# A four-layer graph attention kernel: transposes of x one quad ahead, rows of attention scaled one slot ahead, values a group ahead, last norms in another order

## What is computed

```python
x = _layernorm(x + _L0_gnn_ref(x, adj, ...))   # 4 heads of 64, leaky_relu 0.01, softmax over adj, elu
x = _layernorm(x + _L1_gnn_ref(x, adj, ...))   # 4 heads of 64, leaky_relu 0.2
x = _layernorm(x + _L2_gnn_ref(x, adj, ...))   # 1 head of 256; then three gated dense blocks and two norms
x = _layernorm(x + _L3_gnn_ref(x, adj, ...))   # h = tanh(x W + b); weights exp(h a), masked by adj
# in each: h = x @ W; scores from h; att = softmax(mask(leaky_relu(s_i + s_j))); out = att @ h
```

## Time and profile before

| | |
|---|---|
| median of 3 runs | 3059.14 us (3057.73 to 3062.9) |
| the profiled execution, its own time | 3061.66 us |
| its span | 3059.9 us |
| mean granted clock of PE | 0.993 of full |

### The profile page before, as it was taken

The page is one execution under the profiler, slowest core; times in us unless marked ns, Lnnn a source line. Parts: engine busy times, 40 slices in busy tenths (PEclk is TensorE's granted clock), DMA queues, the critical chain, the costliest instruction groups (busy, mean ns, idle before and its releaser), DMA issues.

```text
span 3059.9 us, 65157 instructions
## 1 busy us (share of the span) xinstructions
PE 2955.5 (97%) x24628; PEld 2582.1 (84%) x24628; DVE 2140.8 (70%) x3855; ACT 1919.1 (63%) x3414; POOL 1174.4 (38%) x1559
## 2 busy tenths in 40 slices
PE   7899999999989999999999999999999999889998
PEld 6899999999979999999997877887778778655555
DVE  5998887888878888888886556665666666562245
ACT  4777898999978999999995545444445444430000
POOL 0661365642226656564121023333323333444222
PEclk9999999999999999999999999999999999989999
DMA  8567100000100000000010000000000000000001
GB/s 286 202 209 250 48 11 11 14 11 15 60 12 14 12 12 13 12 13 11 14 34 12 4 1 4 4 1 4 1 4 4 1 1 1 2 1 1 1 17 39
DMA packets 41912, 104.55 MB, mean 34 GB/s; under 512 B 9856, under 2 KB 23424, under 8 KB 33536
## 3 DMA queue, kind: packets, MB, share of 16 engines
q1 hardware_dynamic: 39616, 101.61, 10.0%
q10 hardware_dynamic: 2112, 0.52, 0.1%
HBM read 97.73 MB, written 4.39 MB: 33 GB/s over the span
## 4 chain that ended last, share of the span: by engine, by line
PE 77%; DVE 3%; ACT 2%; POOL 1%; issue 1%; POOLq 0%; DVEq 0%; ACTq 0%
PE bank L1359 17%; PE bank L1356 16%; PE bank L1414 15%; PE bank L1452 12%; PE bank L1362 10%; PE bank L1441 2%; PE bank L1289 2%; PE bank L1428 1%; PE bank L1569 0%; ACT above L964 0%; DVE rings L1784 0%; ACT rings L1099 0%; DVE rings L1787 0%; ACT values L861 0%; DVE sums L1938 0%
## 5 line engine op out<-in xcount | busy, mean ns | idle before, releaser
L1356 PE MATMUL bank<-values,rings 128*128 128x195 bf16 x8192 | 1414.5, 247 | 37.6 <-DVE rings L1787 25.2
L1359 PE MATMUL bank<-values,rings 128*128 128x195 bf16 x8192 | 1414.6, 249 | 0.0
L964 ACT ACTIVATE above<-srow,kpass 128x512 fp8e4<-128x512 f32 x2032 | 1279.7, 709 | 128.5 <-DVE rings L1787 121.8
L1356 PEld LDWEIGHTS bank<-values,rings 128*128 128x128 fp8e4 x8192 | 806.4, 98 | 47.4 <-issue 45.3
L1359 PEld LDWEIGHTS bank<-values,rings 128*128 128x128 fp8e4 x8192 | 789.1, 96 | 0.6
L1784 DVE TENSOR_TENSOR rings<-rings,above 128x512 uint32<-128x512 uint32 x512 | 400.2, 782 | 192.3 <-PE bank L1359 168.5
L1052 ACT ACTIVATE values<-srow,cmul 128x512 f32<-128x512 f32 x256 | 205.8, 814 | 428.3 <-PE bank L1452 427.3
L1787 DVE TENSOR_TENSOR rings<-rings 128x512 uint32<-128x512 uint32 x512 | 429.7, 839 | 17.3
L1452 PE MATMUL bank<-hv,values 128*128 128x257 f32 x1792 | 420.6, 380 | 0.0
L1452 PEld LDWEIGHTS bank<-hv,values 128*128 128x128 f32 x1792 | 334.9, 190 | 69.9 <-issue 25.2
L1362 PE MATMUL bank<-values,rings 128*128 128x390 bf16 x1920 | 320.3, 329 | 11.9 <-DVE values L1820 11.9
(11 more groups left out here) (223 smaller groups left out, 3479.1 us busy)
## 6 DMA issues: line engine op xcount, KB each, us to landing
arena<-in_adj_dram SPq DMA_DIRECT2D x64, 1024.0 KB, 5.0
srow<-src_dram SPq DMA_DIRECT2D x69, 256.0 KB, 3.2
x<-in_x_dram SPq DMA_DIRECT2D x4, 1024.0 KB, 11.4
out_dram<-x SPq DMA_DIRECT2D x7, 512.0 KB, 2.9
arena<-in_L_gnn_fe_w_dram SPq DMA_DIRECT2D x2, 512.0 KB, 6.7
arena<-in_L_gnn_W_hz_dram SPq DMA_DIRECT2D x1, 1024.0 KB, 7.6
arena<-in_L_gnn_g_w_dram SPq DMA_DIRECT2D x1, 1024.0 KB, 10.8
weights<-in_L_gnn_W_dram SPq DMA_DIRECT2D x3, 256.0 KB, 3.9
```

What stands on the lines that cost most here:

```text
L964: last = act.activation(above[:, k % 2, q, :], srow[:, par, :], ACT.Relu, scale=BIG, bias=kpass[:, p % 2, k * Q + q:k * Q + q + 1], satura ...
L1356: pe.matmul(acc[:, 0:KW], pos[:, k % 2, q, :].bitcast(FP8)[:, rows], v[:, 0:KW], start=start, stop=final, skip_group_check=True)
L1359: last = pe.matmul(acc[:, KW:2 * KW], neg[:, k % 2, q, :].bitcast(FP8)[:, rows], v[:, KW:2 * KW], start=False, stop=final, skip_group_chec ...
```

## The change

Five things move; no arithmetic is added or removed.

1. Layers 0 to 2: a second buffer for the transposed x, and the transposes of quad q+1 (`x_across`) stand between the products of quad q: four after its second tile, four after its fourth. ACT's copies of them (`copy_xT_half`) stand behind the copies of h of the second and fourth tile. PE waits for ACT's copy of h by the tile and no longer by the quad. In layer 1, elu of the last quad and `first_keys` come one quad later.
2. Layer 0: POOL makes the values of the third head one group further ahead of the quotients.
3. Layer 2: `scale_rows` moves on ACT from slot 1, behind `whT`, to slot 0, behind that slot's first rows.
4. End of layer 2: `s_wfix` is signalled before the tail, without waiting for layer 3's vector, which has a semaphore of its own at its first use. The last pair's `g2_product`, `gate_tanh` and `gate_in` come after layer 3's fifth product, its tanh, and `tanh_in(4)`.
5. The end: the first three steps of quad 5's norm come before the last full group's sums, quad 6's first steps after the first addition of `last_rows`, and its last steps between the statistics and the normalising of tile 0 of quad 7.

```diff
-        xT = tiles_room[:, 0:QT * F]
+        xT_rooms = (tiles_room[:, 0:QT * F], tiles_room[:, QT * F + CHUNK * 2 * C:2 * QT * F + CHUNK * 2 * C])
...
+        xT = [xt.rearrange("p (t k n) -> p t k n", t=QT, k=2) for xt in xT_rooms]
...
-        s_wfix = sem("weights_fixed")
+        s_wfix, s_a3 = sem("weights_fixed"), sem("layer3_vector_loaded")
...
                     sp.wait_ge(E.uT, 4 * EG)
-                    load_vector(avec[:, 0, :], A["L3_gnn_a"][:, 0])
+                    sp.dma_start(avec[:, 0, :], A["L3_gnn_a"][:, 0].partition_broadcast(P)).then_inc(s_a3, 16)
...
-        loaded_weights = [16 * 4, 16 * 13, 16 * 16, 16 * 19]
+        loaded_weights = [16 * 4, 16 * 13, 16 * 16, 16 * 18]
...
                 values_of(0, 2, 1)
+                values_of(0, 2, 2)
                 for g in range(2, NG):
-                    values_of(0, 2, g)
+                    if g + 1 < NG:
+                        values_of(0, 2, g + 1)
                     quotient(0, 1, g, g % 2)
...
+                make_rstd(4, QUADS - 3)
                 quotient(3, PASSES[3] - 1, NG - 2, 0)
-                make_rstd(4, QUADS - 3)
                 make_rstd(4, QUADS - 2)
...
-            def copy_quad_xT(l, q):
-                for half in range(2):
-                    act.wait_ge(s_xtps, q * 2 + (l * 2 * QUADS + half + 2))
-                    act.activation(xT[:, 2 * half:2 * half + 2].rearrange("p t k n -> p (t k n)"), bank[half][:, :],
-                                   ACT.Copy).then_inc(s_xt, 1)
+            def copy_xT_half(l, q, half):
+                act.wait_ge(s_xtps, q * 2 + (l * 2 * QUADS + half + 2))
+                act.activation(xT[q % 2][:, 2 * half:2 * half + 2].rearrange("p t k n -> p (t k n)"), bank[half][:, :],
+                               ACT.Copy).then_inc(s_xt, 1)
...
+                    if i % 2 == 1 and q + 1 < QUADS:
+                        copy_xT_half(l, q + 1, i // 2)
...
                         relus(i * SLOTS + slot)
+                        if slot == 0 and i % 2 == 0 and old:
+                            scale_rows(g - 1)
                         if slot == 1 and i > 0:
                             act.wait_ge(E.n1, i + 1)
                             act.activation(whT.rearrange("p k n -> p (k n)"), ps_a, ACT.Copy).then_inc(E.whT, 1)
-                            if old and i % 2 == 0:
-                                scale_rows(g - 1)
...
-                gate_tanh(EG - 1)
                 for r in (4, 5):
                     copy_h(r)
                     copy_xT(r + 2)
                     tanh3(r)
+                    if r == 4:
+                        gate_tanh(EG - 1)
                 copy_h(6)
...
+                    for half in range(2):
+                        copy_xT_half(l, 0, half)
                     for q in range(QUADS):
-                        copy_quad_xT(l, q)
-                        if l == 1 and q + AHEAD + 3 < QUADS:
-                            elu_exp(q + AHEAD + 3)
+                        if l == 1 and q in (0, 2):
+                            elu_exp(AHEAD + 3 + q // 2)
...
+            def x_across(l, q, half):
+                if l == 0 and half == 0 and q % (QUADS // X_PIECES) == 0:
+                    pe.wait_ge(s_x[q // (QUADS // X_PIECES)], 16)
+                for i in (2 * half, 2 * half + 1):
+                    if l > 0:
+                        pe.wait_ge(s_xmade, q * QT + (NORMS[l] * T + i + 1))
+                    for k in range(2):
+                        last = pe.transpose(bank[half][:, (i % 2 * 2 + k) * P:(i % 2 * 2 + k + 1) * P],
+                                            x[:, q * QT + i, k * P:(k + 1) * P], ident[:, :])
+                last.then_inc(s_xtps, 1)
             def dense(l, q):
-                for half in range(2):
-                    for i in (2 * half, 2 * half + 1):
-                        if l > 0:
-                            pe.wait_ge(s_xmade, q * QT + (NORMS[l] * T + i + 1))
-                        for k in range(2):
-                            last = pe.transpose(bank[half][:, (i % 2 * 2 + k) * P:(i % 2 * 2 + k + 1) * P],
-                                                x[:, q * QT + i, k * P:(k + 1) * P], ident[:, :])
-                    last.then_inc(s_xtps, 1)
                 if q == 0:
+                    for half in range(2):
+                        x_across(l, 0, half)
                     pe.wait_ge(s_wfix, l + 1)
-                pe.wait_ge(s_h, q * QT + (l * T + 1))
+                    pe.wait_ge(s_h, l * T + 1)
                 width = F + 2 * H
                 for i in range(QT):
+                    if q > 0:
+                        pe.wait_ge(s_h, (q - 1) * QT + (l * T + i + 2))
                     if l > 0 and q == 0 and 2 + i == GT:
                         pe.wait_ge(s_sums, l * SUMS + 1)
                     pe.wait_ge(s_xt, q * 2 + (l * 2 * QUADS + i // 2 + 1))
                     for k in range(2):
-                        last = pe.matmul(bank[2 + i][:, 0:width], xT[:, i, k, :], weights[:, k, 0:width],
+                        last = pe.matmul(bank[2 + i][:, 0:width], xT[q % 2][:, i, k, :], weights[:, k, 0:width],
                                          start=(k == 0), stop=(k == 1))
                     last.then_inc(s_hps, 1)
+                    if i % 2 == 1 and q + 1 < QUADS:
+                        x_across(l, q + 1, i // 2)
...
-                g2_product(EG - 1)
                 for r in range(4, EG):
                     product3(r)
                     if r + 2 < EG:
                         across3(r + 2)
+                    if r == 4:
+                        g2_product(EG - 1)
...
-                    if l == 1 and q == AHEAD + 1:
+                    if l == 1 and q == AHEAD + 2:
                         first_keys(1)
...
+                chain.enter(NG - 3, 2)
+                for k in (2, 3, 4):
+                    output_norm(QUADS - 3, k)
                 evacuate(3, 0, 0, last_pass + NG - 1)
-                chain.enter(NG - 3, 2)
-                for k in (2, 3, 4, 6, 7):
+                for k in (6, 7):
                     output_norm(QUADS - 3, k)
                 chain.leave(NG - 2)
-                for k in (2, 3, 4, 6, 7):
-                    output_norm(QUADS - 2, k)
                 last_rows()
...
                 link(dve.tensor_tensor(xq, xq, hq, ALU.add))
+                for k in (2, 3, 4):
+                    output_norm(QUADS - 2, k)
                 for it in range(GT):
...
                     dve.bn_aggr(st[:, 6:8], st[:, 0:6]).then_inc(s_var, 1)
+                    if it == 0:
+                        for k in (6, 7):
+                            output_norm(QUADS - 2, k)
                     dve.wait_ge(s_rstd, QUADS * (NORMS[4] + 1) + it)
                     dve.tensor_scalar(tile, tile, st[:, 6:7], st[:, 9:10], ALU.subtract, ALU.mult).then_inc(s_xmade, 1)
...
+                    if r == 0:
+                        dve.wait_ge(s_a3, 16)
...
+                dve.wait_ge(s_w, loaded_weights[3])
+                dve.memset(credits[:, 11:12], 0.0).then_inc(s_wfix, 1)
                 fused_stats(EG - 3)
...
                 g_norm(EG - 2, 0)
-                dve.wait_ge(s_w, loaded_weights[3])
-                dve.memset(credits[:, 11:12], 0.0).then_inc(s_wfix, 1)
                 x_norm(EG - 3)
                 g_norm(EG - 2, 1)
...
                 fused_norm(EG - 2)
+                tanh_in(4)
                 gate_in(EG - 1)
-                tanh_in(4)
                 tanh_scores(4)
```

More of the change, by code:

```diff
@@ L222, in gnn_kernel @@
         tiles_room = vroom[:, T * KW:]
-        xT = tiles_room[:, 0:QT * F]
+        xT_rooms = (tiles_room[:, 0:QT * F], tiles_room[:, QT * F + CHUNK * 2 * C:2 * QT * F + CHUNK * 2 * C])
         vtmp_dve = tiles_room[:, QT * F:QT * F + CHUNK * 2 * C].rearrange("p (a n c) -> p a n c", a=2, c=C)
         ex = [vroom[:, i * QT * F:(i + 1) * QT * F].rearrange("p (t f) -> p t f", t=QT) for i in range(3)]
-        xT = xT.rearrange("p (t k n) -> p t k n", t=QT, k=2)
+        xT = [xt.rearrange("p (t k n) -> p t k n", t=QT, k=2) for xt in xT_rooms]
         class Room:
@@ L1646, in _ @@
                     for q in range(QUADS):
-                        if l == 0 and q % (QUADS // X_PIECES) == 0:
-                            pe.wait_ge(s_x[q // (QUADS // X_PIECES)], 16)
                         dense(l, q)
```

## The result

The median went from 3060.01 us (3057.73 to 3062.9, 4 runs) to 3026.82 (3026.59 to 3030.63, 4 runs), 33.2 us less; the ratio is 0.9894, 95% interval 0.9877 to 0.9911. The forecast was 3029.5, between 3022 and 3039. The profiled execution took 3027.04 us, span 3025.2, mean granted clock 0.992. So the two profiled spans, 3059.86 and 3025.25 unrounded, differ by 34.6 us, against a forecast of 29.6.

What follows compares the result with a forecast made beforehand. PE, busy for 97% of the span, was taken as the bound, so its idle time counts. The terms 3.5 + 4.8 + 0 + 2.9 + 10.5 + 3.4 + 4.5 = 29.6 us gave 3029.5, range 3022 to 3039.

Steps and rivals of the forecast that it cites:

- Layer 2's products: Products of layer 2: transposes between products hide the 0.50 wait for ACT's copy, seven quads, 3.5 us; bounds 2.4 and 4.1.
- Layer 1's products: Products of layer 1: the same 3.5 plus 1.3 from the later elu, 4.8 us; bounds 3.0 and 5.5.
- Layer 0's products: Products of layer 0: nothing gained, as DVE's masks and a conversion waiting for DMA come first; bounds 0 and 3.5.
- Values of the third head: Layer 0's third head: PE's wait for POOL's values goes, 2.9 us; bounds 2.5 and 3.1.
- Layer 2's scaled rows: Layer 2's even pairs: scalings fit ACT's idle time at slot 0, 1.50 us seven times, 10.5; bounds 9.4 and 10.5.
- End of layer 2: Into layer 3: signal ahead of the tail saves wait, overlap and low clock, 3.4 us; gate's move nothing; bounds 0 and 5.
- The end: Last tiles' norms: quads 5 and 6 move forward, PE becomes the bound, 4.5 us; bounds 3.5 and 4.6.
- ACT did not fall behind in layer 1: Rival: ACT falls behind the woven products and layer 1 gives nothing, 4.8 us less, 3034.3; 12 in 100.
- POOL's slower chain: Rival: in layer 2's tail POOL slows beside a busier DVE, nine instructions cost 2.9 us, 3032.4; 15 in 100.
- Layer 0 gained nothing: Rival it answers: layer 0 gains too if DMAs come earlier and masks end before the copies, 3.5 more, 3026.0; 6 in 100.
- The scaling's wait did not move: Rival it answers: layer 2's scaling wait only moves onto ACT's row or whT, 5 us less, 3034.7; 7 in 100.
- The slower rival: Layer 2: ACT stops for late inverses and PE starves; level about 7.5 us late, 3066 at 8.5; 2 in 100 each.

Runs made afterwards that it cites:

- the run with the old places: The changed kernel with first_keys and the last quad's elu at their old places; layer 1's products take 2.7 us longer.
- the two runs above: The kernel before with only the early signal (4.0 us less between layer 2's products and layer 3), or only the values a group ahead (1.7 us less).
- no fill: Fill: the changed kernel plus 47 and 98 throwaway transposes in PE's waits before layer 1's and layer 3's attention; 3023.08 us, ratio 0.9883 to the kernel before.
- three executions: The kernel before, and it with only scaling at slot 0 or only the early signal; the unchanged wait was followed by 2.8, 0 and 1.6 us.
- the run at 8.3: The changed kernel with DVE's inverses at slot 1, each made 17 times in a chain; 3062.81 us, beside 3058.99 of the kernel before.
- At 4.9 us: The changed kernel with DVE's inverses moved from slot 0 to slot 1, behind hs2 and henh; 1.5 us more in layer 2, 0.22 a pair.

## Why the prediction was right, point by point

**Layer 2's products**: right in mechanism, 4.0 for 3.5. Two tiles' products and four transposes take 1605.77 - 1603.56 = 2.21, a quad 4.43 where the earlier trace rows have 5.01; that is 0.58 seven times, the upper bound that the prediction named, since the first product behind a wait also starts slowly (2.02 for 1.95 in the profile above).

**Layer 1's products**: 5.3 for 4.8, by the same 0.5. What is left, 5.3 - 4.0, is the elu's 1.3. What "DVE runs ahead by about as much as PE gains" left open, the run with the old places priced: the woven transposes need both moves, or 2.7 of the 5.3 go.

**Layer 0's products**: right, nothing. PE's last product ended 3.3 us earlier, the attention's first matmul 0.9, and by the ninth group nothing was left.

**Values of the third head**: the wait was right (3.04 for 2.9; the 0.16 of overlap, which the prediction meant to add to each idle figure of PE, is left out of this term), and the trace I compared with had a second loss behind it that I had not looked for. The prediction read that in the earlier trace rows for the other wait and not here. The missed step is the windows behind 498.20 at 0.50. But the fall came in some executions only, so it belongs to a mean over executions with about half its size.

**Layer 2's scaled rows**: right, 10.7 alone for 10.5. The bound of this term was wrong in its reason: 3.3 us of ACT's slack counts for nothing, as ACT's rows are four slots early. What counts is the time to the transposes of the scaled rows, 4.8 us.

**End of layer 2**: 3.7 to 4.0 for 3.4, but by the two runs above only 2.3 of it without a fall of the clock. "Moving the last pair's gate gives nothing" held.

**The end**: 4.6 for 4.5, with PE as the bound, as forecast. The margin was larger than the forecast's 0.8 (3048.8 against 3049.6): DVE stood 1.78 us for PE's last matmul. Without quad 6's move DVE would be the bound.

**The time**: 29.6 forecast, 34.6 in the two profiled executions, 33.2 and 32.7 in the medians. The difference to the medians is 3.1 to 3.6. An estimate of its parts: 0.5 + 0.5 for the products, 0.1 for the third head's overlap, 0.3 for layer 1's first group (28.4 us on average in the four traces with the old order of the products, 28.1 in the eight with the new one and no fill), 0.2 for scaling, 0.1 for the end, and some 1.5 for the falls of the clock at the third head, the mean of three executions. That the time came out 2.7 us from the forecast, inside its range, is not owed to luck: each term is within 0.6 of what its stage gained, and the one cost left out, the low clock at the third head, is small.

**Rivals**: ACT did not fall behind in layer 1 (no wait but the first quad's). The argument against this rival was misread all the same: in layer 2's products ACT was busy for 22.0 of 38.5 us, so it did not idle most of the quad. POOL's slower chain, priced at 2.9, did not show: layer 3 came 14.4 earlier, not 10.5 + 0.5 = 11.0. The last of its nine steps took the longer of the two times, as before:

```profile
2624.48 1.27 POOL L803 TENSOR_TENSOR values<-values 128x512 f32<-128x512 f32 x1
...
2641.14 1.60 POOL L803 TENSOR_TENSOR values<-values 128x512 f32<-128x512 f32 x1
```

All nine together took 8.4 us where they had taken 8.5. Layer 0 gained nothing. The scaling's wait did not move. The slower rival had its point of decision nearly right, level at 7.5 us of lateness where the run at 8.3 is level or a little slower, but from two wrong terms that offset each other: a slack of 3.3 for 4.8, and nothing for the clock where 1.2 a pair was lost. At 4.9 us its price of 1.6 a pair is far off the 0.22 measured.

## What to carry to other kernels

Read PE's granted clock in the windows behind each wait that a change removes, and count what runs at 0.50 there as part of the wait; then see in a second trace of the same kernel whether it is there every time. Price a late producer at the consumer that truly needs it next, not at the next instruction of its queue. When two engines feed a third in one order, moving the transposes ahead pays in full only if the stops of the feeding engines are moved ahead of them too.

## What was not expected of the hardware

The same wait of the same kernel was followed by a fall of the granted clock to 0.50 in one execution and by none in another: 2.88 us of idle time cost 2.8, 0 and 1.6 more, and 1.86 us cost some 1.7 twice and 0 once. Within one execution, that with the later inverses, four of seven waits of 3.44 had the fall and three did not; that is 1.2 each on top, on average. Around the waits of 5.7 and of 11.5 us it came in all twelve traces without fill. The Trainium skill (TensorE: Matmul & The Clock Gate, Part 1) says that the monitor behind the clock runs free of the kernel, so that one kernel sees a different number of slow matmuls by its phase; the three executions of layer 0's third head agree with that, though no run here shows the phase itself.

Transposes of a unit matrix whose result nobody reads kept the clock at 1.00 through an 11.5 us wait: 98 of them took 10.86 us, and the group behind them 21.69 instead of the changed kernel's 23.6.
